# The middle layer's score convolution as 32x32 array blocks

## The reference

```
q, k, v = x @ Wq, x @ Wk, x @ Wv                 # 16 heads of 16
attn = einsum('bhqd,bhkd->bhqk', q, k) * scale
attn0 = where(mask, 0.0, attn).reshape(1, B * H, T, T)
attn = conv_general_dilated(attn0, kernels, (1, 1), padding=((1, 1), (1, 1)), feature_group_count=B * H)
attn = where(mask, -inf, attn)
out = einsum('bhqk,bhkd->bhqd', softmax(attn), v) @ proj_W + proj_b
```

## Time and profile before

| | us |
|---|---|
| median of 3 runs (2318.0 to 2325.0) | 2319.4 |
| span of the profiled execution | 2345.7 |
| the stage `heads1`, in the profile: 584.2 to 1138.6 | 554.4 |
| PE busy over the whole span | 1968.9 |

### The profile page before, as it was taken

One profiled execution on the slowest core, in us unless ns is written; L12 is line 12 of the kernel. 1 busy time (PEld: TensorE's weight loads), 2 busy tenths in 40 slices (PEclk: granted clock), 3 DMA queues, 4 the chain that ended last, 5 costly groups with the idle time before them and its releaser, 6 DMA issues. The chain is left out here.

```text
span 2345.7 us, 41465 instructions
## 1 busy us (share of the span) xinstructions
PE 1968.9 (84%) x13179; PEld 1588.6 (68%) x13201; DVE 1255.6 (54%) x4235; ACT 921.3 (39%) x2196; POOL 776.1 (33%) x1055
## 2 busy tenths in 40 slices
PE   6859999987899999999849988994793797797594
PEld 5747766665798889989749975653582675454593
DVE  2542225633788888888420027975345445784423
ACT  3633321523233333333423345763342344575320
POOL 1012211110444444445211134410555646541132
PEclk9959999988899999999969999995896999899697
DMA  3213221000501110110069964426576475643294
GB/s 138 109 61 124 62 83 43 16 19 23 64 20 33 33 29 20 33 28 2 8 233 342 346 202 113 112 54 252 151 168 244 140 164 121 103 96 121 72 345 141
DMA packets 173404, 261.88 MB, mean 112 GB/s; under 512 B 23184, under 2 KB 138896, under 8 KB 169104
## 3 DMA queue, kind: packets, MB, share of 16 engines
q1 hardware_dynamic: 152272, 209.30, 28.0%
q0 software_dynamic: 16704, 45.64, 8.5%
q10 hardware_dynamic: 4224, 4.33, 0.9%
HBM read 181.19 MB, written 37.75 MB: 93 GB/s over the span
## 5 line engine op out<-in xcount | busy, mean ns | idle before, releaser
L2222 PE MATMUL heads_ps_c<-heads_band,heads_sT 128*128 128x129 f32 x3072 | 370.7, 277 | 13.3 <-DVE heads_band L2447 12.2
L2222 PEld LDWEIGHTS heads_ps_c<-heads_band,heads_sT 128*128 128x128 f32 x3072 | 356.9, 193 | 23.2 <-issue 21.3
L508 POOL DMA_INDIRECT weights_xg<-xn_rows,token_of x197 | 190.3, 966 | 444.8 <-DVE token_of L698 169.9
L2385 POOL TENSOR_SCALAR heads_band<-heads_shifts,heads_taps 128x130 f32<-128x130 f32 x384 | 253.1, 673 | 243.4 <-PE heads_ps_c L2222 239.8
L2315 ACT ACTIVATE heads_probs<-heads_mixes,heads_least 128x256 f32<-128x256 f32 x256 | 116.1, 500 | 344.9 <-DVE heads_least L2460 344.9
L2447 DVE SCALAR_TENSOR_TENSOR heads_band<-heads_shifts,heads_taps,heads_band 128x130 f32<-128x130 f32 x768 | 226.8, 351 | 19.0 <-POOL heads_band L2385 14.4
L1893 ACT ACTIVATE heads_probsT<-heads_ps_e 128x512 f32<-128x512 f32 x256 | 148.0, 597 | 70.0 <-PE heads_ps_e L1736 62.9
L1047 PE MATMUL experts_ps_g<-weights_w,experts_xT 128*128 x504 | 137.1, 396 | 9.1 <-ACT experts_xT L1097 6.9
L1070 PE MATMUL experts_ps_y<-weights_w,experts_hT 128*128 (+1 forms) x486 | 135.2, 387 | 4.3 <-ACT experts_hT L1111 1.7
L1712 PE MATMUL heads_ps_m<-heads_stackK,heads_stackQ 96*128 96x256 bf16 x512 | 101.3, 283 | 31.0 <-DMA heads_stackQ<-heads_q_pieces 12.4
L1104 ACT ACTIVATE experts_silu<-experts_ps_g 128x128 f32<-128x128 f32 (+1 forms) x165 | 53.3, 323 | 162.7 <-PE experts_ps_u L1052 77.8
(11 more groups left out here) (425 smaller groups left out, 4178.9 us busy)
## 6 DMA issues: line engine op xcount, KB each, us to landing
experts_w<-in_experts_dram SPq DMA_DIRECT2D x23, 2180.0 KB
weights_w<-in_experts_dram SPq DMA_DIRECT2D x32, 768.0 KB
weights_w<-in_experts_dram SPq DMA_DIRECT2D x14, 1536.0 KB
y_rows<-experts_y SPq DMA_DIRECT2D x125, 128.0 KB
heads_stackK<-heads_k_pieces SPq DMA_DIRECT2D x192, 64.0 KB, 2.7
heads_stackQ<-heads_q_pieces SPq DMA_DIRECT2D x192, 64.0 KB, 2.5
weights_w<-in_experts_dram SPq DMA_DIRECT2D x8, 1088.0 KB
xn_rows<-xn SPq DMA_DIRECT2D x4, 2048.0 KB, 7.5
```

Source lines behind the costliest of these rows:

```text
L508: pool.indirect_dma_start(self.xg[:, u, :], None, xn_dram, bass.IndirectOffsetOnAxis(ap=tb.token_of[:, j:j + 1], axis=0)).then_inc(self.x_ ...
L2222: last = pe.matmul(out[:, qc * SEQ + k0:qc * SEQ + k1], sT[:, h % 2, kc, qc * P + dq:qc * P + dq + P], band[:, h % 2, dq, w0:w0 + k1 - k0] ...
L2385: last = pool.tensor_scalar(band[:, h % 2, dq, :], shifts[:, 0, :], taps[:, r % 2, h, dq * TAPS:dq * TAPS + 1], None, ALU.mult)
```

## The change

The convolution is turned by its blocks. Scores now have the queries on partitions. The 256 query rows are cut into 9 windows of 30 output rows; a window reads 32 score rows, which fit one 32-row group of the array. Windows 0 to 7 of a head fill 128 partitions twice (`S`); the ninth windows of four heads are packed together (`S_last`). For four heads at a time, `convolve` issues for each of the 3 column taps 16 matmuls of 32x32 weights and 512 columns: row group `i`, column block `j` for head `j`, output in bank `i` of `ps_c`. The ninth windows take three full matmuls (`convolve_last`). Two tap columns are issued back to back, then `convolve_last`, the scores of the third head, and the third tap column; the packed last scores stand behind the fourth head's. `ps_c` takes four banks and is single; scores and projections share `ps_s` (two banks), and turns, mixes and turns back share `ps_t` (two).

POOL builds the bands of four heads at once in six tensor_tensor operations of 384 elements and also splits queries and keys into pieces (four operations of 544 elements a round). DVE no longer touches the bands; it has nine row maxima a quad instead of eight, one more masked copy, and takes the projections out of PSUM. ACT has nine exponentials and nine or ten copies a quad. All loops are written out (no hardware loops). The values are projected from `xnT` itself, so the context copies are gone. The mask is 393 KB, laid out in windows, instead of 131 KB. The inputs of the shared expert are in a stage of their own ("taps"), which ends with one more handover.

```diff
-    for qc in range(QC):
-        for kc in range(QC):
...
-            for dq in range(TAPS):
-                last = pe.matmul(out[:, qc * SEQ + k0:qc * SEQ + k1], sT[:, h % 2, kc, qc * P + dq:qc * P + dq + P],
-                                 band[:, h % 2, dq, w0:w0 + k1 - k0], ...)
+            def score(n, j):
+                u, bank = n // 2, (0, 1, 1, 0)[j]
...
+                if j < 2 and n > 0:
+                    pe.wait_ge(masked, ENTRIES * (n - 1) + GH + j)
+                if j == 0 and n >= 3 and n % 2 == 1:
+                    pe.wait_ge(qk_taken, min((n + 5) // 2, ROUNDS))
+                if j == 1 and n >= 3 and n % 2 == 1:
+                    pe.wait_ge(v_placed, (n + 1) // 2)
...
+            def convolve(n, dk):
+                if dk == 0:
+                    pe.wait_ge(band_ready, n + 1)
+                    pe.wait_ge(masked, ENTRIES * n + GH)
+                for i in range(GROUPS):
+                    rows = slice(LANE * i, LANE * (i + 1))
+                    if dk == 0 and n > 0:
+                        pe.wait_ge(maxed, NW * (n - 1) + 1 + 2 * (i + 1))
+                    for j in range(GH):
+                        last = pe.matmul(ps_c[LANE * j:LANE * (j + 1), i, :], band[rows, n % 2, j, dk, :],
+                                         S[rows, n % 2, j, :, dk:dk + SEQ], start=(dk == 0), stop=(dk == TAPS - 1), ...)
...
+            def convolve_last(n):
+                pe.wait_ge(masked, min(ENTRIES * (n + 1) + 1, ENTRIES * QUADS))
+                for dk in range(TAPS):
+                    last = pe.matmul(ps_s[:, 0, 0:SEQ], band_last[:, n % 2, dk, :, :].rearrange("p j m -> p (j m)"),
+                                     S_last[:, n % 2, dk:dk + SEQ], ...)
+            def turn(n, k):
+                pe.wait_ge(exped, NW * n + k + 1)
+                if k >= 2:
+                    pe.wait_ge(probsT_ready, NW * n + k - 1)
+                elif k == 1 and n > 0:
+                    pe.wait_ge(mixedT_ready, n)
...
+            for n in range(QUADS + 2):
+                ahead, back = n + 1 < QUADS, 1 <= n <= QUADS
+                if ahead:
+                    score(n + 1, 0)
+                    score(n + 1, 1)
+                if n < QUADS:
+                    convolve(n, 0)
+                    convolve(n, 1)
+                    convolve_last(n)
+                if ahead:
+                    score(n + 1, 2)
+                if n < QUADS:
+                    convolve(n, 2)
+                if ahead:
+                    score(n + 1, 3)
+                    score_last(n + 1)
+                if n >= 2:
+                    mix(n - 2)
+                for k in range(NW):
+                    if back:
+                        turn(n - 1, k)
+                    if k == 2 and n % 2 == 1 and n // 2 + 3 < ROUNDS:
+                        pe.wait_ge(masked, ENTRIES * (n + 1) + GH)
+                        project_query_key(n // 2 + 3, 0)
+                    if k == 3 and n % 2 == 1 and n // 2 + 1 < ROUNDS:
+                        pe.wait_ge(masked, ENTRIES * (n + 2))
+                        project_value(n // 2 + 1, 1)
+                if n >= 2:
+                    turn_back(n - 2)
 @block.scalar
+            for n in range(QUADS + 2):
+                for k in range(NW):
+                    if 1 <= n <= QUADS:
+                        exponential(n - 1, k)
+                if n >= 2:
+                    copy_mixed(n - 2)
+                for k in range(NW):
+                    if 1 <= n <= QUADS:
+                        copy_turned(n - 1, k)
...
 @block.gpsimd
+            def make_band(n):
+                if n >= 2:
+                    pool.wait_ge(convolved, GROUPS * (n - 1))
+                    pool.wait_ge(convolved_last, n - 1)
...
+                pool.tensor_tensor(to, tap(0), eye(0), ALU.mult)
+                for a in (1, 2):
+                    last = pool.tensor_tensor(tapped[:, a - 1, :, :, :], tap(a), eye(a), ALU.mult)
...
+                for a in (1, 2):
+                    pool.tensor_tensor(to, to, tapped[:, a - 1, :, :, :], ALU.add).then_inc(tapping, 1)
...
+                pool.tensor_tensor(band_last[...], to, own_rows[...], ALU.mult).then_inc(band_ready, 1)
 @block.vector
+            for n in range(-1, QUADS + 2):
+                if n + 1 < QUADS:
+                    drop_masked(n + 1, 0)
+                    drop_masked(n + 1, 1)
+                if 0 <= n < QUADS:
+                    row_max(n, 0)
+                if n + 1 < QUADS:
+                    drop_masked(n + 1, 2)
+                if 0 <= n < QUADS:
+                    for k in range(1, NW):
+                        row_max(n, k)
+                if n + 1 < QUADS:
+                    drop_masked(n + 1, 3)
+                    drop_masked_last(n + 1)
+                if n >= 2:
+                    finish(n - 2)
+                if n > 0 and n % 2 == 1 and n // 2 + 3 < ROUNDS:
+                    take(n // 2 + 3, 0)
```

More of the change, by code:

```diff
@@ L2069, in conv_heads_stage, with sliding @@
+def sliding(ap, step, count, width):
+    (part, rows), (one, _) = ap.ap
+    return bass.AP(tensor=ap.tensor, offset=ap.offset, ap=[[part, rows], [step * one, count], [one, width]])
+def conv_heads_stage(core, name, xnT, inputs, dst, ident, ones, kernels):
+    ROUNDS, QUADS, STACKS, WB = 2 * B, 4 * B, 2, 3 * DC * D
+    NW, WIDTH = inputs.WINDOWS, inputs.WIDTH
+    GROUPS = 4
+    ENTRIES = GH + 1
+    ORDER = (8, 0, 4, 1, 5, 2, 6, 3, 7)
     stack_dmas = 2 * len(PRODUCTS)
-    def at(i, r):
-        return i + r // SLOTS, r % SLOTS
@@ L2100, in conv_heads_stage @@
[L2100 to L2104, removed]
@@ L2105, in conv_heads_stage @@
-        rows_passed = s.sem("rows_passed")
-        stacked = [s.sem(f"stacked{r}") for r in range(SLOTS)]
-        block = s.block()
[L2109 to L2117, removed]
+        QW, TAIL = NW * LANE, SEQ + 1 - (NW - 1) * WIDTH
+        qk, rest = s.sb("qk", [P, QW + SEQ]), s.sb("rest", [P, QW + SEQ])
@@ L2140, in stack @@
                             .then_inc(stacked[r], 16)
[L2142 to L2154, removed]
@@ new lines, in turn_back @@
+            def turn_back(n):
+                pe.wait_ge(mixedT_ready, n + 1)
+                if n + 1 < QUADS:
+                    pe.wait_ge(probsT_ready, NW * (n + 1) + NW - 1)
+                for c in range(QC):
+                    last = pe.transpose(ps_t[:, n % 2, c * P:(c + 1) * P], mixedT[:, c * P:(c + 1) * P], ident[:, :])
+                last.then_inc(turned_back, 1)
+            pe.wait_ge(w_loaded, 16)
+            project_query_key(0, 0)
+            project_query_key(1, 1)
+            pe.wait_ge(qk_taken, 1)
@@ new lines, in _ @@
+            project_query_key(2, 0)
+            pe.wait_ge(qk_taken, 2)
+            project_value(0, 1)
+            pe.wait_ge(qk_taken, 3)
+            pe.wait_ge(v_placed, 1)
+            for j in range(GH):
+                score(0, j)
+            score_last(0)
+            pe.wait_ge(constants, 1)
+            for n in range(QUADS + 2):
[27 more added lines that the diff above has]
+                    turn_back(n - 2)
@@ L2389, in _ @@
+            make_band(0)
+            split(1)
+            make_band(1)
+            split(2)
+            for n in range(2, QUADS):
+                make_band(n)
+                if n % 2 == 1 and (n - 3) // 2 + 3 < ROUNDS:
+                    split((n - 3) // 2 + 3)
         @block.vector
@@ L2440, in widen_band @@
-            def widen_band(i, H):
-                r, h, n = H // HALF, H % HALF, ALL * i + H
-                v.wait_ge(band_begun, n + 1)
-                for d in range(1, TAPS):
-                    for dq in range(TAPS):
-                        out, tap = band[:, h % 2, dq, :], dq * TAPS + d
-                        last = v.scalar_tensor_tensor(out, shifts[:, d, :], taps[:, r % 2, h, tap:tap + 1], out,
-                                                      ALU.mult, ALU.add)
-                    if d < TAPS - 1:
-                        steps.done(last)
-                last.then_inc(band_ready, 1)
@@ L2483, in loop @@
-            def loop(i, projections):
-                for r in range(SLOTS):
-                    for h in heads(i, r, ((0, drop_masked), (0, widen_band), (1, row_max))):
-                        if r < projections and h in (2, 4, 5, 6, 7):
-                            split(*at(i, r + 3), (2, 4, 5, 6, 7).index(h))
-            for r in range(3):
-                for part in range(5):
-                    split(0, r, part)
-            loop(0, SLOTS)
-            first, per_loop = steps.n, ALL + SLOTS
```

583 lines of the change are left out of this document (277 added, 306 removed).

## The result

| | before | after |
|---|---|---|
| median, us | 2320.42 (4 runs, 2318.0 to 2325.0) | 2257.62 (4 runs, 2253.27 to 2262.92) |
| span of the profiled execution, us | 2345.7 | 2261.2 |
| the stage `heads1`, us | 554.4 | 492.4 (584.9 to 1077.3) |

The ratio is 0.9735 (95% interval 0.9714 to 0.9757), 62.8 us less; 80 were forecast (2240 us). The stage is 62.0 us shorter. The two spans differ by more, 84.5 us, but the profiled span of the kernel before was 25 us over its median and this one 4 us over its own: that difference lies behind the stage, in stages which the change doesn't touch (from the end of `heads1` to the end of the span 1207.1 us before, 1183.9 us after).

A forecast was written before the change was run, and what follows sets the result against it. PE was taken as the bound, through 96 convolution passes, 11.6 of 16.4 us a quad. The stage: 449 + 24 (clock) + 1.5 (handover) = 474.5 us against 554.4, so 2319.4 - 80, predicted 2240 us; range 2205 to 2340.

The forecast's parts named there:

- The convolution, 2.6 us a quad: Convolution passes on PE: 16 blocks run together, 6 rounds of 0.43 us a quad; upper bound 10.3 us.
- Rival 1: Convolution on PE: a block's second pass holds up the next row group, 5.2 us a quad; 2313 us, chance 0.15.
- Rival 2: Convolution on PE: row groups don't run together, 10.3 us a quad for 2.6; 2480 us, slower, chance 0.08.
- Rival 3: Bands and splits: POOL becomes the bound from 1.7 times its 8.1 us a quad; at twice, 2325 us; chance 0.05.
- Rival 4: PE's clock stays at 1.2 GHz for half of the stage: +120 us, 2335 us, chance 0.07.
- case 5: The stage with no loss of clock and turns as priced: 449 us, kernel 2216 us, chance 0.05.
- The steps: PE's chain a quad: 11.3 us, odd steps 14.0, even 13.2; mean 13.6 for 24 steps, 326 us.
- the six changes of shape: Between PE's passes of different block shape in a step: six changes at 0.1 us each, 0.6 us.
- The turns: Nine turns on PE against nine ACT copies, with the mixed copies in front: about 4.6 us a step.
- the wait for `qk_taken`: Even steps: score 0 of an odd quad waits for `take` behind `finish` on DVE, 1.9 us.
- The start: From the stage's start to the first convolution, by projection, split, DMA and scores: 20 us.
- The clock: Stretches at 1.2 GHz in about half of the steps, 1.7 us each over 14: 24 us, bounds 0 to 60.

The follow-up runs named there:

- the repeated set: Changed kernel with each tap column's whole set of 16 blocks issued and then issued again, 192 passes a quad for 96: 2375.8 us, ratio 1.0238.
- the run that repeats inside a row group: Changed kernel with each row group's four column blocks issued twice before the next row group, 192 passes a quad for 96: 2520.55 us, ratio 1.0852.
- the two found so: Taking projections out before `finish` on DVE, against the changed kernel: 2222.41 us; projections behind the sixth turn, against that edit plus paired turns: 2185.13 us.
- the turns with the first of them: Changed kernel with turns in pairs in the halves of a bank and projections taken out before `finish`: 2197.93 us; paired turns alone 2240.56 us.

## Why the prediction was right, and where its terms were off

The kernel takes 2257.62 us for a forecast of 2240, within the 2215 to 2275 that the prediction gave its own case. The stage took 492.4 us for a forecast of 474.5. Of the 17.9 us, 4.0 are the start, 15.4 the steps with the tail (468.4 for 417 + 24 + 12), less the 1.5 of the added handover, which lies outside the stage and which no run measured by itself. No run takes apart the convolution and the other parts of the change (the loops written out, the bands on POOL, the context copies gone); what carries the gain is read from the step.

- **PE was the bound, and the 96 passes of 129 columns were what it cost.** Right: with them gone PE fell from 97.5% to 84%, and the stage by 62 us.
- **The convolution, 2.6 us a quad plus two or three changes of shape.** Mis-sized. It takes 3.36 us from start to start. The prediction took a round of 16 passes to last 0.43 us, like one of four; the repeated set shows 0.55. The Trainium skill ("TensorE: Matmul & The Clock Gate", Part 3) has 10.6 times for 16 tiles, which would make it 3.9. The runs stand between: 16 x 0.43 / 0.55 is 12.5 times.
- **Rival 1, the second pass holding up the next row group.** It falls for this order of calls: 16 passes start within 0.1 us of each other, then the 16 others 0.45 us behind the first. Part of its mechanism shows where a block is asked for again too early (+263 against +118 us). The rule of the Trainium skill ("TensorE: Matmul & The Clock Gate", Part 3), that matmuls start strictly in program order, agrees neither with the two passes of an fp32 call nor, strictly, with the run that repeats inside a row group, where eight passes start together and not four.
- **Rival 2, no row groups together.** It falls: so built, it costs 507 us, of which its 240 are the rounds.
- **Rival 3, POOL.** POOL takes 7.3 us a quad, not 8.1: three of the six operations, those with repeated operands, take 0.84 us, not 1.0, and half a split 1.9, not 2.1. The point from which POOL decides fits, between 14.0 and 17.1 us a quad.
- **Rival 4, half of the stage at 1.2 GHz, and case 5, no loss.** Both fall: the granted clock is 0.94 over the steps.
- **The steps.** 11.78 us for 11.3, and 16.57 for 15.9 (14.0 with the wait of 1.9), which over the 24 middle steps is 14 of the 15 us; the other steps and the tail are 3 us over, the clock 2 to 3 under. In an even step it is the convolution that is over (3.36 for 2.6), of which the six changes of shape, 0.6, cover a part. The turns were right (4.52 for 4.6), the wait for `qk_taken` nearly (1.64 for 1.9; the prediction counts it with the even step, which starts with it). The projection's wait for the fourth masked copy, 0.8 us, had been put at nothing.
- **The start, 20 us.** 24.0, for two reasons in the timeline:

```profile
584.92 8.15 PE L2146 MATMUL heads_ps_s<-xnT,layer_w 128*128 128x256 f32 x24 [1.39 <-PEq L69]
...
590.51 1.40 DVE L2429 TENSOR_TENSOR heads_rest<-heads_qk,heads_pieces 128x544 f32<-128x544 f32 x1
591.95 1.12 DVE L2432 CAST heads_pieces<-heads_rest 128x544 bf16<-128x544 f32 x1
...
603.88 1.01 PE L2177 MATMUL heads_ps_s<-heads_stackK,heads_stackQ 96*128 96x256 bf16 x4 [7.92 <-DMA heads_stackQ<-heads_pieces]
```

  The split on DVE took 4.0 us beside POOL's work at the bands, and the ten microseconds from the first stack transfer (593.85) to the first score are transfers; in the stretch PE's clock is 0.64. No run takes apart what of the start is the split, the transfers and the clock.
- **The clock, 24 us.** Near: 15.4 us go with the wait for `qk`, and at most 6, by its granted clock, with the first 25 us of steps, where stretches at 1.2 GHz remain in every version. What I had not priced is that most of it hangs on that one wait: with it gone the kernel gains nearly twice the wait's own length (37.0 for 19.7).

## What to carry to other kernels

With small blocks of the array, order the calls so that as many different blocks as there are stand one behind the other; a block asked for again too early keeps back others that are free (3.2 us a quad here). When a kernel's bound goes away, read its steps by the distances of the starts, and look for the short waits which remain in the chain: the two found so were worth 33 and 13 us here, and the turns with the first of them more than apart (58 against 48 us). Price a wait with the clock that it may cost behind it, and test an edit that shortens the dense part of a step together with the one that removes the wait.

## What the runs showed of the hardware

- Sixteen 32x32 fp32 passes of 512 columns in 16 different blocks start 6.7 ns apart in the first set of a row, 16.7 ns in the later ones. A round of them takes 0.55 us in a long row, one of four such passes 0.43.
- Called twice inside each row group, 192 such passes take 9.87 us a quad; with the whole set called twice, 6.67. In the first order eight passes start together, in the second sixteen.
- A wait of 1.64 us in every second step brought stretches at 1.2 GHz that cost 15.4 us; with the wait gone there are none.
- The busy share alone doesn't tell the clock. With all passes on one row group PE was busy 95% of the window and the clock was 0.66; in the changed kernel, busy 84%, 0.96; in the kernel before, busy 97%, 0.99. Which activity counts, these runs leave open.
- GpSimd's tensor_tensor of 384 elements with repeated operands takes 0.84 us, with plain ones 1.0.
